# Attention row maxima folded on GpSimd and turned by a DMA through DRAM instead of by TensorE, score stream four units further ahead

## The chip, the core and the metric

One core of a Trainium2 chip runs the whole kernel. The metric is the device time of one execution in microseconds. The kernel before took 1684.84 us, the median of three runs (1678.03 to 1687.31).

## What is computed

One attention layer with a learned scale and offset, a residual layer norm, a linear layer whose input and weight are rounded blockwise to four-bit floats, and another residual layer norm. Batch 2, length 2048, width 256, 16 heads of 16 columns. The part that matters here:

```python
scores = jnp.einsum('bhqd,bhkd->bhqk', Q, K) / sqrt(DK)
scores = scores * tau[..., None] + delta[:, :, None, :]
attn = jax.nn.softmax(scores, axis=-1)
out = jnp.einsum('bhqk,bhkd->bhqd', attn, V)
```

tau and delta are folded into Q and into an extra pair of rows of K, so that one matmul gives the scores.

## The kernel before

The kernel has three stages. The first (0 to about 256 us) makes Q, K and V from x and stores Q and K in DRAM as high and low parts. The second is the attention. The third is the projection, the norms and the four-bit linear layer; a part of it already runs beside the last attention iterations, and the rest is the tail.

The attention runs NIT = 32 iterations. An iteration is one group of four heads (HG) with one chunk of 512 queries; four iterations (NQ) make a group, and at each group's start `group_load` fetches the next group's K and Q into the other half of `k_set` and `q_set`. The softmax needs each row's maximum before the exponent is taken, so the scores are made twice:

- The score stream (`s_unit`, L227) puts 128 queries by 512 keys for two heads into two PSUM banks, and `max_unit` (L237, VectorE) takes the row maxima. There are 32 such units in an iteration's work (UNITS), numbered (j, u) for iteration j. They are the list `items`, in which a few other things are mixed: the item "rows", the item "ft", and twelve output projections O (`block_of`, L867 to L870).
- The transposed scores (`st`, L924) have keys on the partitions. The negated maxima stand as two rows (high and low part) in `q_set`, so that the matmul subtracts them. ScalarE takes the exponent (L1069), and `pv_half` (L937) multiplies it by V.

The order on TensorE is written out by hand. An iteration has 32 slots (SLOTS). In each slot stand one `pv_half`, then one `st` pair for the tile two further on (AHEAD), then the score items that are due. The loop reads:

```python
goal = items.index((i + 2, LEAD)) if i + 2 < NIT else len(items) - 1
due = goal - issued
...
while issued < first + min(due, due * (2 * k + jh + 1) // slots):
    s_item(issued)
```

With LEAD = 12, iteration i ends when 12 units of iteration i + 2 have been issued. An ordinary iteration has 33 items (32 units and one "rows") for its 32 slots, so its last slot has two of them.

The maxima of iteration j go this way: after the last unit VectorE folds the four key chunks (`row_maxima`, L260), GpSimd splits them into high and low parts (`split_max`, L85 and L89), and three units later the item "rows" lets TensorE transpose the 128x128 pad (`rows_turn`, L244) and VectorE copy 32 rows out of PSUM (`rows_copy`, L252). Then SyncE issues four DMAs of 4 KB into `q_set` (`rows_store`, L278). The first `st` of iteration i + 1 is in slot 28 of iteration i and waits for these (`rows_set`).

On ScalarE, `evacuate` (L1058) copies the finished output of an iteration out of PSUM bank 0; the first `pv_half` of the next iteration waits for it (`att_evac`). GpSimd also copies V for the next group (`refill`, L1326) at the quarters of each fourth iteration, and `split_max` stands behind the second of these. It multiplies the output chunks in the end (`normalise`, L1350). SyncE's program in iteration i is: `group_load` (each fourth iteration), `att_store(i - 1)`, loads of output chunks in a few iterations, `rows_store(i + 1)`, and in iteration 30 `z_store(1)` and `next_load(4)` behind it.

In iteration 30 the last 20 units are spread over 24 slots, and slot 24 holds four pairs of unread matmuls (`unread`, L883) and the last "rows".

Of the kernel before, what the change touches and what calls it, by code (L numbers as in the profile page):

```python
# [66 lines left out]
GROUP_DMAS = 2 * (2 * TERMS + 1)  # L67
# [54 lines left out]
def layer_kernel(nc, t, out):  # L122
# [6 lines left out]
    att = dram("att", [NIT, P, CH], F32)  # L129
    z_rows = dram("z_rows", [NCHUNK, HG, HG, CH], F32)  # L130
    rz_rows = dram("rz_rows", [NCHUNK, HG, HG, CH], F32)

    with ExitStack() as top:
# [10 lines left out]
        q_set = sb(top, "q_set", [P, 2, HH, L], F32R)  # L144
# [10 lines left out]
        def group_load(eng, g, done, cols=slice(0, L)):  # L155

            b, h0 = g // (H // HG), g % (H // HG) * HG
            for n in range(GROUP_DMAS):
                half, r = n // (GROUP_DMAS // 2), n % (GROUP_DMAS // 2)
                heads = slice(h0 + HH * half, h0 + HH * (half + 1))  # L160
                base = HALF * half
                if r < 2 * TERMS:
                    dst, src, parts = (k_set, k_parts, K_PARTS) if r < TERMS else (q_set, q_parts, Q_PARTS)
                    r %= TERMS
                    eng.dma_start(dst[base + DK * r:base + DK * (r + 1), g % 2, :, cols].bitcast(F32),
                                  src[parts[r], b, heads, :, cols].rearrange("h d l -> d h l")).then_inc(done, 16)
                else:
                    eng.dma_start(k_set[base + ROW_AUG:base + ROW_AUG + 2, g % 2, :, cols].bitcast(F32),
                                  delta_parts[:, b, heads, cols]).then_inc(done, 16)
# [5 lines left out]
        LEAD = 12  # L175
        DEFER = 3
# [12 lines left out]
        items.append((NIT - 1, "rows"))  # L189
        rows_at = {j: s for s, (j, u) in enumerate(items) if u == "rows"}  # L190
        o_at = {u[1:]: s for s, (j, u) in enumerate(items) if (j, u) in [(k[0], v) for k, v in O_AT.items()]}
        PER = UNITS + 1
        SLOTS = 2 * KT
        s_bank = lambda s: 4 + 2 * (s % 2)
        warm_exp = sb(top, "warm_exp", [P, 1])
        nm = sb(top, "nm", [P, HG * TT])
        nm_pad = sb(top, "nm_pad", [P, P], F32R)
        nm_parts = nm_pad[:, 0:2 * HG * TT].rearrange("p (h t q) -> p h t q", h=HG, t=2)
        nm_rows = sb(top, "nm_rows", [2 * HG * TT, P], F32R)
        nm_max, nm_high, pad_zero, rows_set = sem("nm_max"), sem("nm_high"), sem("pad_zero"), sem("rows_set")  # L200
        ROWS_INC = 16 * HG
# [12 lines left out]
        def s_unit(pe, s):  # L214
# [4 lines left out]
            g, lo = j // NQ, j % NQ * CH  # L219
# [5 lines left out]
            for half in range(2):  # L225
                r = rows_of(half, K_S)
                last = nc.tensor.matmul(ps[:, s_bank(s) + half, :], q_set[r, g % 2, jh, lo + qt * P:lo + (qt + 1) * P],  # L227
# [11 lines left out]
        def rows_turn(pe, s):  # L239

            j, u = items[s]
            pe.wait_ge(s_free, s - 1)
            pe.wait_ge(nm_ready, j + 1)
            nc.tensor.transpose(ps[:, s_bank(s), 0:P], nm_pad[:].bitcast(F32), ident_f[:]).then_inc(s_full, 1)  # L244

        def rows_copy(dve, s):

            j, u = items[s]
            dve.wait_ge(s_full, s + 1)
# [4 lines left out]
        def row_maxima(dve, s):  # L254

            j, u = items[s]
            dve.wait_ge(s_free, s + 1)
            if j > 0:
                dve.wait_ge(nm_ready, j)
            nc.vector.tensor_reduce(nm[:], mx[:, j % 2].rearrange("p a j q c -> p (a j q) c"), AX.X, ALU.max, negate=True).then_inc(nm_max, 1)  # L260
# [1215 lines left out]
```

## Time and profile before

The profiled execution had a span of 1668.4 us from its first to its last instruction. Its whole time was not recorded beside it; the median of the three runs is 1684.84 us.

| | before |
|---|---|
| median of three runs | 1684.84 us |
| span of the profiled execution | 1668.4 us |
| TensorE matmuls busy | 1626.3 us (97%) |
| VectorE busy | 1522.9 us (91%) |
| ScalarE busy | 1311.3 us (79%) |
| GpSimd busy | 128.4 us (8%) |
| mean granted TensorE clock | 0.993 of full speed |
| chain that ended last | PE 59%, VectorE 24% |

L12 means line 12 of the kernel. In a row of the timeline the first number is the start in us from the span's first instruction, the second is how long the group lasted, and `x2` says that two instructions were put together. The square bracket at the end is idle time of the engine before it and what ended it. PE is TensorE, DVE VectorE, ACT ScalarE, POOL GpSimd, SPq SyncE's queue. Matmuls are pipelined and their ends are modelled, so for TensorE the starts are read and not the ends.

### The profile page before, as it was taken

Reading aid. Unit: us, or ns where it says so; the run is one execution under the profiler, and the core shown is the slowest. Engines: PE = TensorE matmul, PEld = TensorE weight load, DVE = VectorE, ACT = ScalarE, POOL = GpSimd, SP = SyncE. Lnnn points to the kernel's source line nnn. Section 1 sums busy time; section 2 is a strip of 40 time slices with the busy share of each in tenths; the row PEclk is TensorE's granted clock in tenths of the full one; section 3 lists DMA queues with packets and bytes.
Section 4 is the critical chain, followed back from the end, with each engine's and each line's share of the span. In section 5 each row is a group of like instructions: output and inputs, shape, how many; then the busy total and the mean of one; then the engine's idle time right before and its main releaser. Section 6 shows DMA issues by size and latency. Waiting matters only on the chain.

```text
span 1668.4 us, 33561 instructions
## 1 busy us (share of the span) xinstructions
PE 1626.3 (97%) x13884; PEld 727.6 (44%) x13884; DVE 1522.9 (91%) x1648; ACT 1311.3 (79%) x2375; POOL 128.4 (8%) x166
## 2 busy tenths in 40 slices
PE   8999998999999999999999999999999999999987
PEld 7766663333333333333333333333333343333466
DVE  5789877999999999999999999999999989898887
ACT  2876737888888888888888888888888876778645
POOL 4222223000000000000000000000010000000100
PEclk9999998999999999999999999999999999999999
DMA  3465426000600060015003300422151001010312
GB/s 113 110 177 157 124 86 122 8 8 9 86 8 8 17 76 8 12 26 70 9 8 41 56 8 8 52 45 53 39 63 30 8 8 40 12 41 10 124 59 89
DMA packets 46960, 84.72 MB, mean 51 GB/s; under 512 B 9116, under 2 KB 21020, under 8 KB 44092
## 3 DMA queue, kind: packets, MB, share of 16 engines
q1 hardware_dynamic: 44952, 82.49, 22.8%
q8 instruction: 109, 1.79, 0.5%
q14 instruction: 43, 0.35, 0.1%
q10 hardware_dynamic: 1856, 0.09, 0.1%
HBM read 51.36 MB, written 30.67 MB: 49 GB/s over the span
## 4 chain that ended last, share of the span: by engine, by line
PE 59%; DVE 24%; issue 1%; ACT 0%; ACTq 0%; POOL 0%; DVEq 0%
PE ps L937 25%; DVE mx L237 20%; PE ps L924 20%; PE ps L227 11%; PE ps L870 1%; DVE stats L1173 1%; PE ps L868 1%; PE ps L244 0%; DVE work L1221 0%; DVE work L1232 0%; PE ps L867 0%; DVE small L1216 0%; DVE mv L1179 0%; DVE scr L1225 0%; DVE work L1229 0%
## 5 line engine op out<-in xcount | busy, mean ns | idle before, releaser
L237 DVE TENSOR_REDUCE mx<-ps 128x2 f32<-128x1024 f32 x1024 | 1228.0, 1222 | 67.9 <-PE ps L227 59.6
L1069 ACT ACTIVATE e<-ps 128x512 f32<-128x512 f32 x2048 | 1109.6, 596 | 220.8 <-PE ps L924 182.7
L937 PE MATMUL ps<-e,v_grp 128*32 128x256 f32 x8192 | 656.1, 392 | 0.3 <-issue 0.3
L924 PE MATMUL ps<-q,k 52*128 52x512 f32 x2048 | 524.7, 499 | 4.1 <-PEq L355 3.8
L227 PE MATMUL ps<-k,q 50*128 50x512 f32 x2048 | 423.6, 405 | 9.5 <-DVE mx L237 6.6
L924 PEld LDWEIGHTS ps<-q,k 52*128 52x128 f32 x2048 | 199.6, 183 | 429.4 <-ACT e L1069 385.9
L937 PEld LDWEIGHTS ps<-e,v_grp 128*32 128x32 f32 x8192 | 161.9, 108 | 354.4 <-issue 204.4
L227 PEld LDWEIGHTS ps<-k,q 50*128 50x128 f32 x2048 | 197.7, 187 | 48.1 <-DVE mx L237 34.3
L684 PE MATMUL ps<-x_p,m_p 128*128 128x512 f32 x576 | 144.2, 404 | 0.0
L525 DVE SCALAR_TENSOR_TENSOR hid<-x_c,dw_w,hid 128x512 f32<-128x512 f32 x128 | 103.7, 860 | 19.0 <-ACT hid L466 19.0
L684 PEld LDWEIGHTS ps<-x_p,m_p 128*128 128x128 f32 x576 | 107.0, 190 | 31.8 <-issue 7.3
L472 ACT ACTIVATE hid<-hid 128x512 f32<-128x512 f32 x64 | 40.5, 632 | 52.3 <-DVE hid L525 51.0
L85 POOL CAST nm_pad<-nm 128x16 fp32r<-128x16 f32 x32 | 6.7, 210 | 871.7 <-DVE nm L260 871.7
L466 ACT ACTIVATE hid<-x_c,dw_b,dw_w 128x512 f32<-128x512 f32 x64 | 46.6, 804 | 0.2
L1326 POOL COPY v_grp<-v_all 128x272 f32<-128x272 f32 x32 | 13.7, 433 | 316.8 <-PE ps L937 316.8
L870 PE MATMUL ps<-wo_t,v_all 128*128 128x256 f32 x128 | 32.8, 379 | 0.0
L707 PE MATMUL ps<-hid,pw_w 128*16 128x512 f32 x128 | 30.2, 594 | 0.1
L1350 POOL TENSOR_TENSOR v_all<-v_all 128x1024 f32<-128x1024 f32 x8 | 20.3, 2540 | 117.5 <-DMA v_all<-rz_rows 117.5
L515 ACT ACTIVATE q_sp<-qx 128x512 fp32r<-128x512 f32 x16 | 10.1, 630 | 21.3 <-DVE qx L549 21.1
L698 PE MATMUL ps<-wv_p,x_p 128*128 128x256 f32 x192 | 26.8, 289 | 0.0
L990 PE MATMUL ps<-fw_p,xq_t 128*128 128x256 f32 x128 | 19.6, 310 | 7.0 <-ACT xq_t L1051 7.0
L89 POOL TENSOR_TENSOR q_sp<-qx,q_sp 128x512 fp32r<-128x512 f32 x16 | 20.5, 1282 | 73.6 <-ACT q_sp L515 73.5
(142 smaller groups left out, 623.5 us busy)
## 6 DMA issues: line engine op xcount, KB each, us to landing
k<-k_parts SPq DMA_DIRECT2D x42, 256.0 KB
q<-q_parts SPq DMA_DIRECT2D x42, 256.0 KB
k_parts<-k_sp SPq DMA_DIRECT2D x16, 512.0 KB, 4.9
q_parts<-q_sp SPq DMA_DIRECT2D x16, 512.0 KB, 3.8
att<-ev SPq DMA_DIRECT2D x32, 256.0 KB
x_c<-in_x_t SPq DMA_DIRECT2D x8, 514.0 KB, 5.3
tau_r<-tau_rows SPq DMA_DIRECT2D x16, 256.0 KB
x_in<-in_x SPq DMA_DIRECT2D x8, 512.0 KB, 3.9
```

What stands on the lines that cost most here:

```text
L227: last = nc.tensor.matmul(ps[:, s_bank(s) + half, :], q_set[r, g % 2, jh, lo + qt * P:lo + (qt + 1) * P], k_set[r, g % 2, jh, kc * CH:(kc ...
L237: nc.vector.tensor_reduce(mx[:, j % 2, :, jh, qt, kc], ps[:, b0:b0 + 2, :], AX.X, ALU.max).then_inc(s_free, 1)
L466: nc.scalar.activation(hid[:, k, c, r], x_c[:, n % 2, c, 1:1 + CH], ACT.Identity, bias=dw_b[:, k, c, r:r + 1], scale=dw_w[:, k, c, r, 1:2] ...
L472: nc.scalar.activation(hid[:, k, c, r], hid[:, k, c, r], ACT.Gelu).then_inc(gelu_done, 1)
L525: nc.vector.scalar_tensor_tensor(y_, x_c[:, n % 2, c, which:which + CH], dw_w[:, k, c, r, which:which + 1], y_, ALU.mult, ALU.add).then_in ...
L684: mm = nc.tensor.matmul(ps[:, o, :], m_p[:, kw, side, c, tap, P * o:P * (o + 1)], x_p[:, n % 2, kx_, c, tap:tap + CH], start=(m == 0), sto ...
L698: last = nc.tensor.matmul(ps[:, v_bank(n, v), D * a:D * (a + 1)], x_p[:, n % 2, kx_, c, lo:lo + P], wv_p[:, kw, c, :], start=(m == 0), sto ...
L707: last = nc.tensor.matmul(ps[32 * k:32 * k + H, TD_BANK, :], pw_w[:, k, 2 * c + r, :], hid[:, k, c, r, :], start=(j < 2), stop=(j >= 6))
L870: last = nc.tensor.matmul(dst, a_t[p][:, c, P * a:P * (a + 1)], wo_t[:, c, :], start=False, stop=(c == CT - 1))
L924: nc.tensor.matmul(ps[:, st_bank(n), :], k_set[r, g % 2, jh, kt * P:(kt + 1) * P], q_set[r, g % 2, jh, lo:lo + CH], start=True, stop=True) ...
L937: last = nc.tensor.matmul(ps[32 * h:32 * (h + 1), 0, PVW * part:PVW * (part + 1)], v_grp[:, kt, h, :], e[:, x % E_BUFS, h * CH + PVW * par ...
L1069: nc.scalar.activation(e[:, x % E_BUFS, h * CH:(h + 1) * CH], ps[:, st_bank(n), :], ACT.Exp).then_inc(e_ready, 1)
```

## The change

The item "rows" goes away, with its transpose on TensorE, its copy on VectorE and the fold on VectorE. GpSimd folds the four maxima of each row with small `tensor_scalar` instructions on 128x1 columns (`FOLD_ORDER`: eight places, four instructions each, and a wait in each place), then splits high and low as before into a pad of 128x32. One DMA writes the pad to DRAM turned, that is in 4096 runs of four bytes, and after waiting for it SyncE issues two DMAs that read 8 KB each back into `q_set`, whose layout becomes [rows, group, chunk, head, 512] so that these two rows are contiguous. `group_load` now has one DMA for each head of Q, in all 20 DMAs instead of 14 for a group. LEAD goes from 12 to 16. Iteration 30 spreads its units over 20 slots, without the unread matmuls. `z_reciprocal(1)` moves behind two small aggregations.

```diff
-        LEAD = 12
-        DEFER = 3
+        LEAD = 16
...
-                if u == DEFER - 1 and j > 0:
-                    items.append((j - 1, "rows"))
...
+        def split_max(pool, j):
+
+            folds = 2 * HH * TT * j
+            for qt, jh in FOLD_ORDER:
+                pool.wait_ge(s_free, unit_at[j, qt, jh, NQ - 1] + 1)
+                for half in range(2):
+                    r, parts = (half * HH + jh) * TT + qt, mx[:, j % 2, half, jh, qt]
+                    nc.gpsimd.tensor_scalar(mn[:, r:r + 1], parts[:, 0:1], parts[:, 1:2], parts[:, 2:3], ALU.max, ALU.max).then_inc(mx_folded, 1)
+                folds += 2
+                pool.wait_ge(mx_folded, folds)
+                for half in range(2):
+                    r, parts = (half * HH + jh) * TT + qt, mx[:, j % 2, half, jh, qt]
+                    nc.gpsimd.tensor_scalar(nm[:, r:r + 1], mn[:, r:r + 1], parts[:, 3:4], -1.0, ALU.max, ALU.mult).then_inc(nm_max, 1)
+            pool.wait_ge(nm_max, folds)
             if j > 0:
-                dve.wait_ge(rows_set, j * ROWS_INC)
-            nc.vector.tensor_copy(nm_rows[:], ps[0:2 * HG * TT, s_bank(s), 0:P]).then_inc(s_free, 1)
...
+                pool.wait_ge(rows_out, 16 * j)
+            cols = nm[:].rearrange("p (a r) -> p a r", a=2)
             high(nc.gpsimd, nm_parts[:, :, 0], cols).then_inc(nm_high, 1)
             pool.wait_ge(nm_high, j + 1)
             low(nc.gpsimd, nm_parts[:, :, 1], cols, nm_parts[:, :, 0]).then_inc(nm_ready, 1)
 
         def rows_store(sp, j):
 
-            sp.wait_ge(s_free, rows_at[j] + 1)
-            g, lo = j // NQ, j % NQ * CH
-            for h in range(HG):
-                row = HALF * (h // HH) + ROW_MAX
-                sp.dma_start(q_set[row:row + 2, g % 2, h % HH, lo:lo + CH].bitcast(F32).rearrange("t (a l) -> t a l", a=TT),
-                             nm_rows[h * 2 * TT:(h + 1) * 2 * TT, :].bitcast(F32)).then_inc(rows_set, 16)
+            sp.wait_ge(nm_ready, j + 1)
+            g = j // NQ
+            sp.dma_start(max_rows[j].rearrange("r p -> p r"), nm_pad[:].bitcast(F32), allow_slow_non_contiguous=True).then_inc(rows_out, 16)
+            sp.wait_ge(rows_out, 16 * (j + 1))
+            for half in range(2):
+                row = HALF * half + ROW_MAX
+                sp.dma_start(q_set[row:row + 2, g % 2, j % NQ].bitcast(F32),
+                             max_rows[j, BLOCK // 2 * half:BLOCK // 2 * (half + 1)].rearrange("(t j q) p -> t j (q p)", t=2, j=HH)).then_inc(rows_set, 16)
...
-                        if s == len(items) - 1:
-                            pe.wait_ge(s_free, s - 1)
-                            unread(s_bank(s), 4)
-                        if u == "rows":
-                            rows_turn(pe, s)
-                        else:
-                            s_unit(pe, s)
+                        s_unit(pe, s)
...
-                        goal = items.index((i + 2, LEAD)) if i + 2 < NIT else len(items) - 1
+                        goal = items.index((i + 2, LEAD)) if i + 2 < NIT else len(items)
                         due = goal - issued
-                        slots = SLOTS * 3 // 4 if i == NIT - 2 else SLOTS
+                        slots = SLOTS * 5 // 8 if i == NIT - 2 else SLOTS
```

## Rows read from the trace of the kernel before

**Rows 1.** The page: the chain that ended last, shares of the span by engine.
```profile
PE 59%; DVE 24%; issue 1%; ACT 0%; ACTq 0%; POOL 0%; DVEq 0%
```

**Rows 2.** Instructions of line L1058 up to 1200 us: count, ns min/median/max, first and last start.
```profile
L1058 ACT ACTIVATE ev<-ps x23: 602/603/604, 303.8 to 1194.0; 128x512 f32<-128x512 f32 x23
```

**Rows 3.** Timeline of TensorE, iteration from 627.6 to 667.85: start us, us, what.
```profile
656.09 0.64 PE L937 MATMUL ps<-e,v_grp 128*32 128x256 f32 x8
...
657.35 0.64 PE L937 MATMUL ps<-e,v_grp 128*32 128x256 f32 x8
...
658.59 0.64 PE L937 MATMUL ps<-e,v_grp 128*32 128x256 f32 x8
659.16 0.51 PE L924 MATMUL ps<-q,k 52*128 52x512 f32 x2
659.50 0.41 PE L227 MATMUL ps<-k,q 50*128 50x512 f32 x2
...
666.03 0.64 PE L937 MATMUL ps<-e,v_grp 128*32 128x256 f32 x8
...
666.93 0.98 PE L227 MATMUL ps<-k,q 50*128 50x512 f32 x4
667.85 0.64 PE L937 MATMUL ps<-e,v_grp 128*32 128x256 f32 x8
```

**Rows 4.** Timeline of VectorE, an ordinary iteration and a stretch with a backlog.
```profile
658.70 35.28 DVE L237 TENSOR_REDUCE mx<-ps 128x2 f32<-128x1024 f32 x29 [0.96 <-PE ps L227]
...
1377.87 9.24 DVE L237 TENSOR_REDUCE mx<-ps 128x2 f32<-128x1024 f32 x8 [0.43 <-PE ps L227]
```

**Rows 5.** Timeline of ScalarE where two iterations meet.
```profile
666.92 0.60 ACT L1058 ACTIVATE ev<-ps 128x512 f32<-128x512 f32 x1
```

**Rows 6.** Timeline of TensorE, iteration 30: two slots that hold one score unit.
```profile
1514.38 0.64 PE L937 MATMUL ps<-e,v_grp 128*32 128x256 f32 x8
...
1516.85 0.64 PE L937 MATMUL ps<-e,v_grp 128*32 128x256 f32 x8
```

**Rows 7.** Timeline of TensorE, iteration 31: two slots without any score item.
```profile
1573.55 0.64 PE L937 MATMUL ps<-e,v_grp 128*32 128x256 f32 x8
...
1575.80 0.64 PE L937 MATMUL ps<-e,v_grp 128*32 128x256 f32 x8
```

**Rows 8.** Timeline of TensorE, iteration 30: the last "rows" slot, then an output projection.
```profile
1536.68 0.64 PE L937 MATMUL ps<-e,v_grp 128*32 128x256 f32 x8
...
1539.21 0.64 PE L937 MATMUL ps<-e,v_grp 128*32 128x256 f32 x8
...
1542.43 0.28 PE L867 MATMUL ps<-bias,ones 128*128 128x256 bf16 x1
...
1543.94 0.64 PE L937 MATMUL ps<-e,v_grp 128*32 128x256 f32 x8
```

**Rows 9.** The page: DMA queues, with packets, MB and share of 16 engines' span.
```profile
q1 hardware_dynamic: 44952, 82.49, 22.8%
q10 hardware_dynamic: 1856, 0.09, 0.1%
```

**Rows 10.** Instructions of tile z (loads of 32 KB from DRAM): issue to landing.
```profile
DMA to landing us min/median/max: 1.7/1.8/2.9
```

**Rows 11.** Timeline of GpSimd, iteration 3, which began at 385.25.
```profile
404.57 0.43 POOL L1326 COPY v_grp<-v_all 128x272 f32<-128x272 f32 x1 [9.49 <-PE ps L937]
411.70 0.20 POOL L85 CAST nm_pad<-nm 128x16 fp32r<-128x16 f32 x1 [6.69 <-DVE nm L260]
411.98 0.23 POOL L89 TENSOR_TENSOR nm_pad<-nm,nm_pad 128x16 fp32r<-128x16 f32 x1
```

**Rows 12.** Busy us of each engine at a group load's end; clock, DMA share, GB/s last.
```profile
445.00:450.00 5.00, 5.00 (x50) 1.82 (x48) 4.74 (x5) 4.17 (x9) 0.00 (x0) 1.00 0.54 98
```

**Rows 13.** Timeline of TensorE, iteration 31: the first block of projection 4.
```profile
1558.56 0.27 PE L867 MATMUL ps<-bias,ones 128*128 128x256 bf16 x1 [1.04 <-issue]
```

**Rows 14.** Timeline of VectorE, the start of the tail.
```profile
1597.62 0.76 DVE L1173 BATCH_NORM_STATS2 stats<-ps 128x6 f32<-128x256 f32 x2 [5.28 <-PE ps L870]
```

More of the change, by code:

```diff
@@ L66 @@
 THREE = ((0, 0), (0, 1), (1, 0))
-GROUP_DMAS = 2 * (2 * TERMS + 1)
+GROUP_DMAS = 2 * (TERMS + HH * TERMS + 1)
 def chain(eng, sem, base=0):
@@ L188, in layer_kernel @@
                     items.append((j, O_AT[j, u]))
-        items.append((NIT - 1, "rows"))
-        rows_at = {j: s for s, (j, u) in enumerate(items) if u == "rows"}
+        FOLD_ORDER = [(qt, jh) for qt in range(TT) for jh in range(HH)]
         o_at = {u[1:]: s for s, (j, u) in enumerate(items) if (j, u) in [(k[0], v) for k, v in O_AT.items()]}
-        PER = UNITS + 1
         SLOTS = 2 * KT
@@ L195, in layer_kernel @@
         warm_exp = sb(top, "warm_exp", [P, 1])
+        mn = sb(top, "mn", [P, HG * TT])
         nm = sb(top, "nm", [P, HG * TT])
[L197 to L201, printed above, removed]
+        nm_pad = sb(top, "nm_pad", [P, BLOCK], F32R)
+        nm_parts = nm_pad[:].rearrange("p (a t r) -> p a t r", a=2, t=2)
+        mx_folded, nm_max, nm_high, rows_out, rows_set = sem("mx_folded"), sem("nm_max"), sem("nm_high"), sem("rows_out"), sem("rows_set")
+        ROWS_INC = 16 * 2
         mx = sb(top, "mx", [P, 2, 2, HH, TT, NQ])
@@ L226, in s_unit @@
                 r = rows_of(half, K_S)
-                last = nc.tensor.matmul(ps[:, s_bank(s) + half, :], q_set[r, g % 2, jh, lo + qt * P:lo + (qt + 1) * P],
+                last = nc.tensor.matmul(ps[:, s_bank(s) + half, :], q_set[r, g % 2, j % NQ, jh, qt * P:(qt + 1) * P],
                                         k_set[r, g % 2, jh, kc * CH:(kc + 1) * CH], start=True, stop=True)
@@ L712, in pre_scores @@
                     for s in pre_at.get((n, place), ()):
-                        if items[s][1] == "rows":
-                            rows_turn(pe, s)
-                        else:
-                            s_unit(pe, s)
+                        s_unit(pe, s)
                 beta(1, 0)
@@ L876, in loaded @@
                         pe.wait_ge(a_norm, n + 1)
-                    def unread(bank, pairs):
-                        for m in range(pairs):
-                            for half in range(2):
-                                r = rows_of(half, K_S)
-                                nc.tensor.matmul(ps[:, bank + half, :], q_set[r, (NG - 1) % 2, 0, 0:P], k_set[r, (NG - 1) % 2, 0, 0:CH], start=True, stop=True)
                     def s_item(s):
@@ L1012, in _ @@
                                     issued += 1
-                                if i == NIT - 2 and 2 * k + jh == slots:
-                                    s_item(len(items) - 1)
                             if x in PROJECT_AT:
```

72 lines of the change are left out of this document (22 added, 50 removed).

## The prediction, made before the changed kernel was run

> **What bounds the kernel now.** I read the page first. Its busy shares, 97% for TensorE and 91% for VectorE, are too near each other to decide anything; the chain that ended last gives 59% to the one and 24% to the other [rows 1]. The copies of the finished output mark the iterations: 23 of them from 303.8 to 1194.0 us, so 890.2 / 22 = 40.46 us for an iteration [rows 2]. The timeline of TensorE says what one is made of. A slot with one score unit lasts 658.59 - 657.35 = 1.24 us, the slot with the transpose 657.35 - 656.09 = 1.26, and the last slot, which has two units, 667.85 - 666.03 = 1.82 [rows 3]. The sum 30 x 1.24 + 1.26 + 1.82 = 40.28 is the iteration.
>
> Is VectorE the pace of the 1.24? Its 29 reduces in 35.28 us are 1.217 each, nearly without idle time, and look like a bound. But where it has a backlog, eight take 9.24 us, 1.155 each [rows 4]. It could do 32 reduces in 37.0 us. So VectorE follows TensorE, except in the two-unit slot, where the second pair stands 0.5 us behind the first (four matmuls last 0.98 us where a pair lasts 0.41 [rows 3]), since a PSUM pair comes free only after a reduce. What the change takes from VectorE (a fold and a copy for each iteration) is therefore worth nothing by itself in the ordinary iterations. What counts is TensorE's list of slots.
>
> **The edge between iterations.** One item fewer makes 32 items for 32 slots, and no slot has two. I don't take that as 1.82 down to 1.24, for the next `pv_half` also waits for the output copy: it starts at 666.92 and takes 0.60, to 667.52 [rows 5]. With 0.05 for the handover (an assumption, no row gives it) TensorE could go on at 667.57 and not at 667.85. So the edge slot becomes 667.57 - 666.03 = 1.54, a gain of 0.28. Its bounds are 0, should something else hold it, and 0.58. The transpose slot becomes a plain one and gives 0.02. That is 0.30 an iteration, at most 0.6, at least 0.02.
>
> **The sum over iterations.** I worked out from the two lists how many items fall in each iteration.
> - Iterations 1 to 23: 33 items become 32. 23 x 0.30 = 6.9 us gained.
> - Iteration 0: 36 items become 38 because of LEAD, four two-unit slots become six. An extra one costs 1.82 - 1.24 = 0.58. Lost: 1.2.
> - Iteration 24 loses one two-unit slot (34 to 33, 0.6) and iteration 25 is ordinary (0.3). Gained: 0.9.
> - Iteration 26 gets a second output projection and loses "rows". A projection takes 1543.94 - 1542.43 = 1.51 in its slot [rows 8], where a score pair takes 1.24 - 0.91 = 0.33 [rows 3]. Lost: 1.2.
> - Iterations 27 and 28: 37 become 36, one two-unit slot fewer each, with VectorE near its limit. Gained: 0.9 each (0.6 from TensorE's side, 1.2 if a reduce's whole time counts), 1.8.
> - Iteration 29: 36 become 34 with one projection fewer. Two two-unit slots (1.2) and a projection (1.2). Gained: 2.4.
> - Iteration 30: the slot with the unread matmuls and the last transpose took 1539.21 - 1536.68 = 2.53 [rows 8] and becomes one without a score item. Leaving a unit out of a slot gives nothing while every second slot has one: 1516.85 - 1514.38 = 2.47 for two slots with one unit [rows 6], the same as 2 x 1.24, since ScalarE then catches up. Only where no units are left is a slot shorter, 2.25 / 2 = 1.12 [rows 7]. The last units end in slot 19, not 23, so four slots at 0.12 and one at 1.4. Gained: 1.9.
> - The tail gives nothing. It begins where VectorE had been idle 5.28 us for the last projection but two [rows 14], so it moves with TensorE.
> - The first stage has 42 units in place of 41 and a transpose ahead of the attention, 0.1 us. The new `rows_store(0)` there blocks SyncE for some 5 us ahead of two stores, whose data GpSimd and ScalarE give later anyway. Nothing.
>
> Together 6.9 - 1.2 + 0.9 - 1.2 + 1.8 + 2.4 + 1.9 = 11.5 us gained, if nothing comes late.
>
> **Does the new path come in time?** The slots are counted from an iteration's start. The first `st` of the next iteration stands in slot 28, 28 x 1.24 = 34.7 us in, and 659.16 - 658.59 = 0.57 behind the slot's start (the score pair is 0.91 behind it) [rows 3]. So the rows are due at 35.3 us.
>
> *The last unit.* With LEAD = 16 it is in slot 15: 15 x 1.24 + 0.91 = 19.5, matmul 0.4 [rows 3], reduce 1.2 [rows 4], so its maxima stand at 21.2.
>
> *GpSimd.* The trace shows no fold of 128x1 there. The nearest rows are a cast of 128x16 at 0.20 and the instruction that waits for it, 0.28 behind [rows 11]. Two folds, a wait and two folds I put at 0.75; it may be 0.45 or, if reading two scalars from SBUF is slow, 1.3. The last place then ends at 21.9, and high and low add 0.6: 22.6. The other seven places are done by then. What is queued behind the waits on GpSimd is the refill for the next group, and there the order matters: in iterations 3, 7, ... 27 `split_max` stands behind the second refill, which began 404.57 - 385.25 = 19.3 in and took 0.43 [rows 11]. All eight places come after 19.8, so 19.8 + 8 x 0.75 + 0.6 = 26.5 (24.0 to 30.8).
>
> *The DMA out.* 4096 runs over 16 engines are 256 for each. No row shows it. The nearest is queue 10, which moved small pieces: 0.1% of 16 engines' span is 26.7 us for 1856 packets, 14 ns each, and by the rounding 7 to 22 [rows 9]. The far end is queue 1, 22.8% for 44952 packets of 1.8 KB, 135 ns each. With 1.7 us for what any small DMA takes [rows 10] the DMA is 5.4 us, between 3.5 and 36. I take 5.4, since queue 10's packets are the nearest in size, and see its own spread of 3.5 to 7.4 as likely.
>
> The Trainium skill, "DMA: Bandwidth & Descriptors", gives about 10.5 ns for a packet (Measured) and about 2 us fixed (Anatomy of one DMA), so an estimate of 2.0 + 256 x 10.5 ns = 4.7 us; the sum would be the same by it.
>
> *The two DMAs in.* An issue of 0.6 each and a landing of 1.8 behind the second's start [rows 10]: 2.4.
>
> So an ordinary iteration has its rows at 22.6 + 5.4 + 2.4 = 30.4, due 35.3; the DMA out may take up to 10.3. A group's last iteration has them at 34.3, and the DMA out may take up to 6.4. In iteration 30 the last unit is in slot 19, four slots later, 5.0 us: rows at 35.4 against 20 x 1.24 + 8 x 1.12 + 0.57 = 34.3. That one is late by 1.1 us. SyncE, blocked meanwhile, has behind it `z_store(1)` and `next_load(4)`, for whose outcome TensorE waited 1.04 us already [rows 13]; but by this reckoning it comes free at 34.2, about a microsecond sooner than now. I charge 1.0 for iteration 30.
>
> *Queues.* The load of group 2 kept the DMA engines busy for 0.54 of the stretch from 445 to 450 [rows 12], so it ended about 447.7. The iteration began at 385.25 + 40.3 = 425.5, so that is 22.2 us in; its bytes stay, its Q pieces shrink from 8 to 2 KB. The DMA out would be issued at 22.7, right behind. Should the load grow by two or three of the 4.9 us to spare there, nothing is late. The 20 issues for 14 are 3 us more of SyncE, beside the transfers.
>
> Total: 11.5 - 1.0 = 10.5 us gained. The span of 1668.4 becomes 1657.9. The change touches nothing outside the span, so I take the same off the median: 1684.8 - 10.5 = 1674.3 us.
>
> **Rivals.**
> - *Late at the groups' ends only.* The DMA out takes about 8.5 us, or the folds 1.1 a place. Then 8.5 - 6.4 = 2.1 us in seven iterations is 14.7, and iteration 30 loses 4.2 and not 1.0. In all 11.5 - 18.9 = 7.4 lost: 1692. With 7.5 us it is 11.5 - 7.7 - 3.2 = 0.6 gained: 1684. For it: 256 little writes to DRAM for each engine are seen nowhere in the trace. Against it: queue 10.
> - *The DMA out is slow everywhere, and the kernel slower.* The place is `rows_out` on SyncE, the point from which it decides is 10.3 us (34 ns a piece). At 13 us it costs 2.7 x 23 = 62 in ordinary iterations, 6.6 x 7 = 46 at the groups' ends and 8.7 in iteration 30, so 105 lost and 1790. Beyond it every microsecond costs 31. The row for it is queue 1 with 135 ns a packet, against it that those are big packets. The skill's page "DMA: Bandwidth & Descriptors" speaks against the change here: a strided last dimension becomes one descriptor for each element, and its rules for kernel authors call a plain DMA with a rearranged pattern, as a transpose, 19 times slower than the hardware's. No run here shows that ratio.
> - *The edge gives nothing.* Something else keeps the edge at 1.82, or the chain through ScalarE's copy shifts. Then 0.28 x 25 = 7.0 fall away: 3.5 gained, 1681.
>
> **How the numbers follow.** Forecast, in time nearly everywhere: 0.57, with 1668 to 1679 for its own range (edge gain 0.58 at one end, iteration 0 and the projections worse at the other, and the spread of the runs). Late at the groups' ends: 0.16. Slow everywhere: 0.14. Edge gives nothing: 0.13. The range must leave out the slow case and little more: 1667 to 1693. About 0.5%, 8.4 us, is what a measurement of this kernel can tell from no change. Below 1676.4 lies some three quarters of the forecast's case: 0.44. Above 1693.3 lie the slow case and a part of the late one: 0.18. Between them 0.38.
>
> **What would show each step.** In the profile after: two starts of L937 across an edge 1.54 us apart, ordinary iterations of 40.0 us, no pair of units in a slot. VectorE with idle time in each slot's end, which costs nothing. GpSimd with 32 small instructions an iteration, 0.75 us a place. The DMA out at 5.4 us between its issue and the issues of the two DMAs in. The wait of the first `st` in slot 28 absent, but for iteration 30. I am wrong if that wait shows in iterations 3, 7, ... 27 (late folds or DMA), or in all, or if slots without two units last longer than 1.24.

## The result: 2067 us, a fifth slower

The changed kernel takes 2067.40 us, the median of four runs (2059.09 to 2095.76), beside 1685.64 us (1678.03 to 1687.31), the median of four for the kernel before. The ratio is 1.228, with a 95% interval of 1.2237 to 1.2326; the slow one of the four, 2095.76 us at a lower granted clock, is left out of it. The forecast was 1674.3 us with a range of 1667 to 1693, so both were wrong. The case that happened is the rival "the DMA out is slow everywhere", to which I had given 0.14 and a price of 1790 us.

| | before | after |
|---|---|---|
| median of four runs | 1685.64 us | 2067.40 us |
| span of the profiled execution | 1668.4 us | 2057.2 us |
| TensorE matmuls busy | 1626.3 us (97%) | 1767.3 us (86%) |
| VectorE busy | 1522.9 us (91%) | 1525.1 us (74%) |
| GpSimd busy | 128.4 us (8%) | 450.6 us (22%) |
| mean granted TensorE clock | 0.993 | 0.871 |

The page of the changed kernel: number of packets, then the chain that ended last by engine and by line. Line numbers are those of the changed kernel: L264 is the DMA out, L268 the two in, L891 `st`, L904 `pv_half`, L225 the score units.
```profile
DMA packets 182614, 85.29 MB, mean 41 GB/s; under 512 B 141628, under 2 KB 152508, under 8 KB 181084
...
PE 32%; DMA 27%; DVE 19%; POOL 6%; issue 1%; ACT 1%; SPq 0%; POOLq 0%; ACTq 0%; DVEq 0%
DMA max_rows<-nm_pad 24%; DVE mx L235 16%; PE ps L904 14%; PE ps L891 11%; PE ps L225 6%; DMA q<-max_rows 4%; POOL mn L246 3%; POOL nm L251 2%; PE ps L850 1%; DVE stats L1133 1%; PE ps L848 1%; SPq L268 0%; POOL nm_pad L89 0%; POOL nm_pad L85 0%; DVE work L1192 0%
```
In [rows 1] no DMA stood in the chain. Now the DMA out alone has 24% of it. The group of `st` on the page shows the wait (busy us, mean ns, then idle time before it and what ended it):
```profile
L891 PE MATMUL ps<-q,k 52*128 52x512 f32 x2048 | 577.0, 545 | 255.1 <-DMA q<-max_rows 243.5
L904 PE MATMUL ps<-e,v_grp 128*32 128x256 f32 x8192 | 723.2, 428 | 1.1 <-ACT ev L1023 0.8
```
One ordinary iteration, 592.20 to 641.16 us, shows how it goes. SyncE's queue:
```profile
615.80 0.38 SPq L264 DMA_DIRECT2D max_rows<-nm_pad  x1
630.96 0.53 SPq L268 DMA_DIRECT2D q<-max_rows  x2
```
The DMA out is issued 23.6 us into the iteration, and the two DMAs in follow 15.16 us later. Over the 32 iterations this distance is 14.65 to 17.2 us, median 15.75. TensorE, where the iteration's first `st` for the next iteration stands:
```profile
626.04 0.64 PE L904 MATMUL ps<-e,v_grp 128*32 128x256 f32 x8
...
627.51 0.64 PE L904 MATMUL ps<-e,v_grp 128*32 128x256 f32 x8
633.53 0.79 PE L891 MATMUL ps<-q,k 52*128 52x512 f32 x2 [5.38 <-DMA q<-max_rows]
634.68 1.08 PE L904 MATMUL ps<-e,v_grp 128*32 128x256 f32 x8
...
636.85 1.08 PE L904 MATMUL ps<-e,v_grp 128*32 128x256 f32 x8
...
639.00 1.08 PE L904 MATMUL ps<-e,v_grp 128*32 128x256 f32 x8
```
The wait is 5.38 us, and the slots behind it last 636.85 - 634.68 = 2.17 us and not 1.24. The same stretch by engine busy time; the last three columns are granted clock, DMA share and GB/s:
```profile
616.00:618.00 2.00, 2.00 (x24) 0.68 (x22) 1.97 (x3) 1.86 (x4) 0.00 (x0) 1.00 0.48 8
...
622.00:624.00 2.00, 2.00 (x24) 0.61 (x20) 1.97 (x3) 1.69 (x5) 0.00 (x0) 1.00 0.22 0
...
626.00:628.00 2.00, 2.00 (x22) 0.79 (x20) 1.75 (x3) 1.80 (x4) 0.00 (x0) 1.00 0.00 0
...
633.00:638.00 5.00, 4.47 (x26) 1.55 (x26) 2.27 (x2) 2.17 (x4) 0.00 (x0) 0.50 0.00 1
638.00:643.00 5.00, 5.00 (x28) 1.75 (x28) 2.63 (x3) 2.77 (x5) 0.00 (x0) 0.50 0.14 54
643.00:648.00 5.00, 5.00 (x46) 1.58 (x44) 4.11 (x4) 3.95 (x8) 0.00 (x0) 0.88 0.00 0
```
Three things are to be seen. The packets of the DMA out are over by 626, yet SyncE is released only at 631: the records of its packets end long before the DMA counts as done. Nor are these records long. From 614 to 634 us the queue that carries it shows (packets, MB, share of 16 engines' time):
```profile
q1 hardware_dynamic: 4120, 0.03, 17.3%
```
That is 0.173 x 16 x 20 us / 4120 = 13.4 ns a packet, next to the 14 ns that the prediction took from queue 10. By its packet records the DMA out is as cheap as forecast; what takes the time is not in them. And behind the wait TensorE has a granted clock of 0.50, 1.2 GHz in place of 2.4, up to about 644 (0.88 is the mean of a stretch that begins at 0.50).

### The profile page after: what moved, and what is told of

Its sections match the earlier page's. It is cut to its first block, busy times and chain, and to the rows that moved or that the text cites. A ratio compares the mean times of both kernels' runs of the same rounds, so it can differ in the third digit from the quotient of the medians.

```text
span 2057.2 us, 34377 instructions
## 1 busy us (share of the span) xinstructions
PE 1767.3 (86%) x13839; PEld 763.4 (37%) x13844; DVE 1525.1 (74%) x1584; ACT 1315.1 (64%) x2375; POOL 450.6 (22%) x1189
## 4 chain that ended last, share of the span: by engine, by line
PE 32%; DMA 27%; DVE 19%; POOL 6%; issue 1%; ACT 1%; SPq 0%; POOLq 0%; ACTq 0%; DVEq 0%
DMA max_rows<-nm_pad 24%; DVE mx L235 16%; PE ps L904 14%; PE ps L891 11%; PE ps L225 6%; DMA q<-max_rows 4%; POOL mn L246 3%; POOL nm L251 2%; PE ps L850 1%; DVE stats L1133 1%; PE ps L848 1%; SPq L268 0%; POOL nm_pad L89 0%; POOL nm_pad L85 0%; DVE work L1192 0%
## 5 line engine op out<-in xcount | busy, mean ns | idle before, releaser
L235 DVE TENSOR_REDUCE mx<-ps 128x2 f32<-128x1024 f32 x1024 | 1241.7, 1224 | 429.3 <-PE ps L225 417.4
L891 PE MATMUL ps<-q,k 52*128 52x512 f32 x2048 | 577.0, 545 | 255.1 <-DMA q<-max_rows 243.5
L904 PE MATMUL ps<-e,v_grp 128*32 128x256 f32 x8192 | 723.2, 428 | 1.1 <-ACT ev L1023 0.8
L891 PEld LDWEIGHTS ps<-q,k 52*128 52x128 f32 x2048 | 218.1, 199 | 747.0 <-ACT e L1034 446.3
L225 PE MATMUL ps<-k,q 50*128 50x512 f32 x2048 | 458.1, 438 | 6.5 <-DVE mx L235 6.2
L246 POOL TENSOR_SCALAR mn<-mx 128x1 f32<-128x1 f32 x512 | 182.4, 365 | 698.8 <-DVE mx L235 676.1
L904 PEld LDWEIGHTS ps<-e,v_grp 128*32 128x32 f32 x8192 | 168.4, 112 | 413.2 <-issue 269.9
L225 PEld LDWEIGHTS ps<-k,q 50*128 50x128 f32 x2048 | 221.4, 209 | 32.4 <-DVE mx L235 18.8
L251 POOL TENSOR_SCALAR nm<-mn,mx 128x1 f32<-128x1 f32 x512 | 141.5, 290 | 25.2
L1286 POOL COPY v_grp<-v_all 128x272 f32<-128x272 f32 x32 | 13.5, 428 | 502.1 <-PE ps L904 502.1
L89 POOL TENSOR_TENSOR q_sp<-qx,q_sp 128x512 fp32r<-128x512 f32 x16 | 20.5, 1280 | 73.9 <-ACT q_sp L503 73.7
L89 POOL TENSOR_TENSOR x_p<-x_c,x_p 128x1028 fp32r<-128x1028 f32 x8 | 19.3, 2415 | 63.2 <-ACT x_p L448 63.1
L1023 ACT ACTIVATE ev<-ps 128x512 f32<-128x512 f32 x32 | 19.1, 598 | 15.6 <-PE ps L904 15.6
```

What stands on the lines that cost most here:

```text
L235: nc.vector.tensor_reduce(mx[:, j % 2, :, jh, qt, kc], ps[:, b0:b0 + 2, :], AX.X, ALU.max).then_inc(s_free, 1)
L246: nc.gpsimd.tensor_scalar(mn[:, r:r + 1], parts[:, 0:1], parts[:, 1:2], parts[:, 2:3], ALU.max, ALU.max).then_inc(mx_folded, 1)
L251: nc.gpsimd.tensor_scalar(nm[:, r:r + 1], mn[:, r:r + 1], parts[:, 3:4], -1.0, ALU.max, ALU.mult).then_inc(nm_max, 1)
L891: nc.tensor.matmul(ps[:, st_bank(n), :], k_set[r, g % 2, jh, kt * P:(kt + 1) * P], q_set[r, g % 2, i % NQ, jh, :], start=True, stop=True). ...
L904: last = nc.tensor.matmul(ps[32 * h:32 * (h + 1), 0, PVW * part:PVW * (part + 1)], v_grp[:, kt, h, :], e[:, x % E_BUFS, h * CH + PVW * par ...
```

## The experiments

All are edits of the changed kernel but for three, where that is said. "DMA out" is the distance from its issue to the issue of the first DMA in behind it, median of the 32; a slot is the distance between two successive groups of eight `pv_half` matmuls. A slot is called long when it is 0.8 to 1.1 us over 1.24 after all waits of its `st` are taken off. Where no range stands, the time is that of one run.

### 1. The same bytes in runs of 128

```diff
-            sp.dma_start(max_rows[j].rearrange("r p -> p r"), nm_pad[:].bitcast(F32), allow_slow_non_contiguous=True).then_inc(rows_out, 16)
+            sp.dma_start(max_rows[j].rearrange("r p -> (r p)").rearrange("(p r) -> p r", p=P), nm_pad[:].bitcast(F32)).then_inc(rows_out, 16)
...
-                                nc.scalar.activation(e[:, x % E_BUFS, h * CH:(h + 1) * CH], ps[:, st_bank(n), :], ACT.Exp).then_inc(e_ready, 1)
+                                nc.scalar.activation(e[:, x % E_BUFS, h * CH:(h + 1) * CH], ps[:, st_bank(n), :], ACT.Exp, scale=2.0**-10).then_inc(e_ready, 1)
```

> The changed kernel with one thing other: the DMA out writes each partition's 32 maxima as one run of 128 bytes (128 runs), not turned, so that the two DMAs in fetch misplaced maxima; the exponent's scale is lowered so that it stays finite. All counts of instructions and bytes stay. Theory: the four-byte writes are the whole loss. Then DMA out to the next issue falls from 15.2 us to 1.7 to 2.5, ordinary iterations come to 40.0 us with an edge of 1.54, and the groups' last iterations are about 1 us late, since eight places of 1.43 us on GpSimd end at 31.9 us. Time 1674 plus 7 x 1 us, and up to 7 x 5 more if the TensorE clock falls after such a wait: 1675 to 1715. Rival: a part of the loss is in the rest of the change (more DMAs for the group load, folds on GpSimd, 16 units ahead): then well above 1715.

Measured: 1664.41 us (1662.9 to 1670.38) beside 1677.37, ratio 0.9915 (0.9886 to 0.9944). SyncE's queue in one iteration, then the copies of the finished output up to 1200 us:
```profile
651.84 0.35 SPq L264 DMA_DIRECT2D max_rows<-nm_pad  x1
653.28 0.54 SPq L268 DMA_DIRECT2D q<-max_rows  x2
```
```profile
L1023 ACT ACTIVATE ev<-ps x23: 603/603/603, 306.8 to 1190.0; 128x512 f32<-128x512 f32 x23
```
The DMA out takes 653.28 - 651.84 = 1.44 us, no `st` waits for rows, and an iteration lasts (1190.0 - 306.8) / 22 = 40.15 us in the mean, against 40.46 in [rows 2]. So the whole loss, 2057.2 - 1662.5 = 394.7 us of span, comes from the shape of one DMA of 16 KB. GpSimd's folds, the blocked SyncE, the finer loads of Q and the longer lead together cost nothing that shows here. That wrong maxima pass through this kernel does not explain it: experiment 7, whose result is right, has the same iterations.

The 394.7 us can be taken apart by slots. From the first to the last slot the changed kernel takes 1724.6 us and this one 1330.8, 393.8 more. Of these, 248.5 are waits of `st`: 243.5 for rows, the others for ScalarE. 115.1 - 4.7 = 110.4 are long slots (125 of them against 5), the 2.17 us slots above. The rest, 35, are smaller and larger lengthenings.

### 2. The size of the runs

The same 16 KB in 2048 runs of 8 bytes, again not turned. In this, in 3 and in 5 the exponent has the scale of experiment 1.

```diff
+            sp.dma_start(max_rows[j].rearrange("r p -> (r p)").rearrange("(r p w) -> p r w", p=P, w=2), nm_pad[:].bitcast(F32).rearrange("p (r w) -> p r w", w=2)).then_inc(rows_out, 16)
```

> The changed kernel with 2048 runs of eight bytes in place of 4096 of four (misplaced maxima, lowered exponent scale). If each little write has its price, about 57 ns on its engine, the DMA out falls from 15.2 us to about 8.5 and the ordinary iterations meet their due time or miss it by little: 1690 to 1760. If the price is by bytes or is fixed for a turned pattern, it stays at 15 us and the time above 2000.

Measured: 1726.14 us, DMA out 7.28. The first `st` waits only where a group of heads ends, 4.5 to 5.0 us in six of them and 2.2 in iteration 27, and 1.7 us in iteration 30 (the waits of TensorE: us in total, times, longest):
```profile
PE ps L891 <- DMA q<-max_rows: 32.5, 8, 5.0
```
This puts a point between the two thresholds of the prediction, 6.4 and 10.3 us: 7.28 us is in time in ordinary iterations and late at the groups' ends.

### 3. Four bytes, 64 bytes apart

The contiguous DMA of experiment 1 feeds the kernel, and beside it the pad goes out turned as in the change, but each run to a 64-byte piece of its own.

```diff
+            sp.dma_start(max_far[j, :, :, 0].rearrange("r p -> p r"), nm_pad[:].bitcast(F32), allow_slow_non_contiguous=True).then_inc(rows_out, 16)
```

> The changed kernel, but the 4096 runs of four bytes go to places 64 bytes apart in another DRAM tensor, and a contiguous copy beside it feeds the DMAs in (misplaced maxima, lowered exponent scale). Rival theory: the writes are slow since sixteen of them, from different engines, hit the same 64-byte piece of DRAM. By it the DMA out falls from 15 us to below 8. By the theory of a price for each write it stays at 15 to 16 us, time 2040 to 2100.

Measured: 1741.14 us, 8.22 us for both DMAs (6.3 to 10.4), waits of 5.5 to 7.5 us at the groups' ends (2.4 at the last). As many runs as in the changed kernel, of the same size, take half the time once no two share 64 bytes. No other spacing was run, and the runs are also spread over sixteen times as much memory, so that 64 bytes is the size that counts is not shown.

### 4. The turn on the way in

The pad goes out contiguous, and four DMAs of 1024 four-byte pieces each read it turned. Nothing is left out.

```diff
-                sp.dma_start(q_set[row:row + 2, g % 2, j % NQ].bitcast(F32),
...
+                for part in range(2):
+                    c0 = BLOCK // 2 * half + BLOCK // 4 * part
+                    sp.dma_start(q_set[row + part:row + part + 1, g % 2, j % NQ].bitcast(F32).rearrange("t j (q p) -> t (j q) p", p=P),
+                                 max_rows[j, :, c0:c0 + BLOCK // 4].rearrange("p r -> r p").unsqueeze(0), allow_slow_non_contiguous=True).then_inc(rows_set, 16)
```

> The changed kernel with the turn on the other side: out as 128 runs of 128 bytes, and in by four DMAs whose 1024 pieces of four bytes each are read from DRAM with a stride and written to SBUF in order, on eight engines, so 512 for an engine. The result is the full one. If a four-byte write to DRAM is the dear thing and a four-byte read and a write into SBUF are cheap (7 to 14 ns), out takes 2 us and in 6 to 10 us, and the time is 1675 to 1720. If any four-byte piece costs 57 ns, in takes 29 us and the time goes beyond 2200.

Measured: 2260.57 us. `st` waits 450.2 us in all, and the issues alone hold SyncE for 10 us:
```profile
PE ps L893 <- DMA q<-max_rows: 450.2, 32, 22.6
```
```profile
654.37 0.32 SPq L264 DMA_DIRECT2D max_rows<-nm_pad  x1
655.78 10.27 SPq L270 DMA_DIRECT2D q<-max_rows  x4
```
The first `st` behind these came at 676.29, 20.5 us behind the first issue. Reading in four-byte pieces is no way out.

### 5. Neighbours written one behind the other

After experiment 3 my theory was that several DMA engines meet in one 64-byte piece of DRAM. Here each partition's 128 bytes are meant to be written by one engine, in order, still as 4-byte runs. For this the pad in SBUF holds its values 8 bytes apart, so the reading side changes too.

```diff
-        nm_pad = sb(top, "nm_pad", [P, BLOCK], F32R)
-        nm_parts = nm_pad[:].rearrange("p (a t r) -> p a t r", a=2, t=2)
+        nm_pad = sb(top, "nm_pad", [P, BLOCK, 2], F32R)
+        nm_parts = nm_pad[:, :, 0].rearrange("p (a t r) -> p a t r", a=2, t=2)
...
-            sp.dma_start(max_rows[j].rearrange("r p -> p r"), nm_pad[:].bitcast(F32), allow_slow_non_contiguous=True).then_inc(rows_out, 16)
+            sp.dma_start(max_rows[j].rearrange("r p -> (r p)").rearrange("(p r) -> p r", p=P), nm_pad[:, :, 0].bitcast(F32), allow_slow_non_contiguous=True).then_inc(rows_out, 16)
```

> The changed kernel with 4096 runs of four bytes, read with a stride of eight from the pad and written in order, so that each partition's 128 bytes of DRAM are written by one engine (misplaced maxima, lowered exponent scale). Runs to places 64 bytes apart took 8.2 us with the copy beside them, runs next to each other from several engines 15.8. If the second half of the price comes from several engines writing one 64-byte piece, this one takes 6 to 8.5 us and the time is 1710 to 1760. If it comes from writing the same piece sixteen times by whatever engine, it stays at 14 to 16 and the time above 2000.

Measured: 2516.8 us, the slowest of all. SyncE's queue, and three of the stretches behind the issue (last columns: clock, DMA share, GB/s; a share can pass 1, since the records of packets overlap):
```profile
658.07 0.56 SPq L264 DMA_DIRECT2D max_rows<-nm_pad  x1
687.55 0.53 SPq L268 DMA_DIRECT2D q<-max_rows  x2
```
```profile
663.00:668.00 5.00, 5.00 (x52) 1.83 (x48) 4.94 (x5) 4.38 (x9) 1.25 (x4) 1.00 1.58 1
...
673.00:678.00 5.00, 0.00 (x0) 0.00 (x0) 0.00 (x0) 0.00 (x0) 0.00 (x0) 0.66 0.05 0
678.00:683.00 5.00, 0.00 (x0) 0.00 (x0) 0.00 (x0) 0.00 (x0) 0.00 (x0) 0.50 0.00 0
```
The theory fell. As the DMA is written, no 64-byte piece is shared between engines (the trace does not name the engine of a packet), and it takes 28.75 us, not less. From 678 us on no packet is in the records, nearly ten of the 29.5 us of this one. With the contiguous 1.44 us taken off, and the runs taken as spread evenly over 16 engines, the price of one run on its engine is:

| what is written | runs per engine | DMA out | ns a run |
|---|---|---|---|
| 4 B, next run in the same 64 B (this one) | 256 | 28.75 us | 107 |
| 4 B turned (the change) | 256 | 15.75 us | 56 |
| 8 B (experiment 2) | 128 | 7.28 us | 46 |
| 16 B (experiment 7) | 64 | 3.15 us | 27 |
| 4 B, 64 B apart (experiment 3; 0.38 us for the second issue taken off too) | 256 | 8.22 us | 25 |

So the price is not one of a packet's passage. Among the four-byte runs it is lowest where no two share 64 bytes and highest where they follow each other into the same 64. What in the memory path does it stays open, and for the 107 ns so does the part of the spaced reading from SBUF, which was not tried alone. The Trainium skill, "DMA: Bandwidth & Descriptors" (Specifications), says that below 512 bytes the DMA reads, modifies and writes. That would fit a run that has to wait for its neighbour, but it doesn't by itself tell 25 ns from 107, and no run here shows the reading.

### 6. The late start on GpSimd

In the iterations that end a group, the eight folds stand behind the second refill. This takes that away, with all work kept.

```diff
-                            if c == 2 and i + 1 < NIT:
+                            if c == 0 and i + 1 < NIT:
```

> The changed kernel with GpSimd's fold and split put ahead of the refills for the next group instead of behind the second one. Theory: in iterations 3, 7, ... 27 the eight places, 1.43 us each, stand behind a refill that begins at 19.3 us, which makes the stall 15 us there instead of 5.5. Then those seven stalls fall to 5 to 6 us and the time by 7 x 9.5 = 66 us, to 1985 to 2015. Rival: the DMA out is later there for another cause, and the time stays above 2050.

Measured: 2033.48 us. The waits at the groups' ends fall to about 6 us, as long as those of ordinary iterations:
```profile
PE ps L891 <- DMA q<-max_rows: 187.7, 32, 10.2
```
That is 243.5 - 187.7 = 55.8 us less waiting, near the 66 expected, but only 25.6 us less span, so the time missed its range. The long slots rose from 115.1 to 147.3 us; two traces of the changed kernel itself differ by 21 (136.2 in experiment 9). So the mechanism of the wait is right, and shorter waits did not bring fewer slots at the lower clock.

### 7. Sixteen bytes, the turn half done by the matmul

From the kernel before. A unit takes the queries 4p + qt and not qt * 128 + p, by a strided read of its weights, so four maxima of a partition lie together in a row and the DMA out has 1024 runs of 16 bytes. The fold stays on VectorE, LEAD is 14, nothing is left out.

```diff
-                last = nc.tensor.matmul(ps[:, s_bank(s) + half, :], q_set[r, g % 2, jh, lo + qt * P:lo + (qt + 1) * P],
+                last = nc.tensor.matmul(ps[:, s_bank(s) + half, :], q_set[r, g % 2, jh, lo:lo + CH].rearrange("r (p q) -> r p q", q=TT)[:, :, qt],
...
+            sp.dma_start(max_rows[j].rearrange("r p q -> p r q"), nm_pad[:].bitcast(F32).rearrange("p (r q) -> p r q", q=TT)).then_inc(rows_out, 16)
```

> A kernel of its own, full result: the kernel before without the item rows; VectorE folds as before; unit qt takes the queries 4p + qt (weights read with a stride of 16 bytes), so that a partition's four maxima are neighbours in the row and the turn through DRAM needs 1024 runs of 16 bytes; LEAD = 14, last units over 20 slots. If a little write costs 46 to 57 ns, 64 for each engine are 3 to 3.7 us and the DMA out is 4.4 to 5.1, in time everywhere. The slots are those of the contiguous run, less one two-unit slot in iteration 0: 1660 to 1668, 0.85% to 1% below the kernel before. Against it: if the strided weights load slower than the matmul before hides, each slot grows from 1.24 and the time is above 1690.

Measured: 1668.01 us (1666.4 to 1672.04) beside 1679.17, ratio 0.9935 (0.9914 to 0.9956).
```profile
658.16 0.37 SPq L255 DMA_DIRECT2D max_rows<-nm_pad  x1
661.36 1.25 SPq L259 DMA_DIRECT2D q<-max_rows  x2
```
The DMA out takes 3.15 us in the median, no `st` waits for rows, ordinary iterations last 40.0 us, and a slot is 1.24 with the strided weights as without. This kernel is 0.65% below the kernel before, a small gain but clear of the noise, and far below the changed one.

### 8. Its lead, and the lead alone

The same with LEAD = 12:

> The variant with runs of 16 bytes, with the score stream at the changed kernel's least lead that still covers the rows: 12 units in place of 14. Its two DMAs take 3.15 us out and about 2 in where the rows would then land some 32.6 us into an iteration and are wanted at 35.3. Theory: nothing waits in ordinary iterations, the first iteration saves two slots (1.2 us), and the time is 1664 to 1670 us, as with 14. Rival: at the ends of the groups of heads the rows come 4 us later and now too late; then a wait of about 1.3 us and the clock behind it, in 7 iterations, 1678 to 1690 us.

Measured: 1673.12 us (1668.64 to 1676.31) beside 1676.78, ratio 0.9968 (0.9948 to 0.9987). No wait for rows in ordinary iterations or at groups' ends, as the theory had it, but no gain either; against 0.9935 the intervals overlap.

And the kernel before with its lead changed and nothing else:

```diff
-        LEAD = 12
+        LEAD = 16
```

> The kernel before with LEAD = 16 and nothing else: the score stream four units ahead, the turn still on TensorE. Iteration 0 has 40 items for 36 and pays 4 x 0.58 = 2.3 us; the last iterations get back as much; the edge keeps its two units. Expected the same within 0.3% of the kernel before. If the stream's lead were the gain seen with the contiguous DMA (14 us), it would show here.

Measured: 1675.48 us beside 1679.17, ratio 0.9977 (0.995 to 1.0004): no difference that can be told.

### 9. Is the rest the clock?

The changed kernel with matmuls that nobody reads ahead of the wait for the rows, in two sizes, and once as it is.

```diff
+                            if i > 0:
+                                n_next = filler_at[0]
+                                pe.wait_ge(s_free, min(n_next, len(items)) - 1)
+                                for m in range(62 if i % NQ == 0 else 22):
+                                    for half in range(2):
+                                        r = rows_of(half, K_S)
+                                        nc.tensor.matmul(ps[:, s_bank(n_next) + half, :], q_set[r, g % 2, 0, 0, 0:P], k_set[r, g % 2, 0, 0:CH], start=True, stop=True)
```

First with 45 and 15:

> The changed kernel, all of its work kept, with matmuls that nobody reads put in front of the wait of the first st for its rows (15 pairs in an ordinary iteration, 45 where a new group of heads begins), so that TensorE computes while the rows are on their way. In the changed kernel that wait takes 4.5 to 7.8 us in an ordinary iteration and 13.5 to 15.5 at a group's first, 244 us in all, and beside it some 150 us more are lost against the kernel with runs of 128 bytes. Theory: these 150 us are TensorE at 1.2 GHz after each idle wait (slots of 2.16 us at a granted clock of 0.50 where 1.24 is usual). Then the slots behind the wait stay at 1.24 us, the period of an ordinary iteration falls from 49 to 52 us to about 46, and the time to 1920 to 1950 us. Rival: the slots are long for another reason, the rows' packets in the DMA engines or a backlog of VectorE; then the filled wait changes nothing and the time stays at 2040 or above.

Measured: 2076.59 us, so by the letter the rival's number. But the trace says something else than the rival: the mean clock rose to 0.916, the long slots fell from 115.1 to 79.5 us, and the DMA out took 17.62 us and not 15.75, which is 1.9 x 31 = 59 us by itself. The fill was too short as well. This was inconclusive, hence two more (the 77 us of the second text are these 79.5, counted with only the wait for the rows taken off):

> The changed kernel as it is, on the same chip as the run with the longer filled wait beside it. With 15 and 45 pairs of unread matmuls ahead of the wait, the DMA out took 17.6 us in place of 15.75 and the time did not fall. If that is the chip it ran on, the DMA out of the changed kernel is about 17 us here and its time 2100 us or more. If the unread matmuls lengthen it, it is 15 to 16.5 us here and the time 2060 to 2075 us.

> The changed kernel with 22 pairs of unread matmuls ahead of the wait in an ordinary iteration and 62 at a group's first (15 and 45 before), enough to cover nearly the whole wait. At 0.43 us a pair they take 9.5 and 26.7 us, more than the waits of the changed kernel, so the time is no lower: 2030 to 2110 us. What is asked is the clock. Theory (the slots of 2.16 us follow from the idle wait): with 15 and 45 pairs 77 us were left in slots 0.8 to 1.1 us too long, after 115 in the changed kernel and 5 in the kernel with runs of 128 bytes; now under 20 us are left, and the mean granted clock is 0.97 or more. Rival: such slots come with the scattered DMA whether TensorE waits or not; then 60 us or more of them stay.

Measured on one chip: the changed kernel 2072.98 us with a DMA out of 15.56, the one with the filled wait 1971.73 us with 15.70. TensorE of the latter in an ordinary iteration, and its clock there:
```profile
610.20 0.64 PE L911 MATMUL ps<-e,v_grp 128*32 128x256 f32 x8
610.90 5.30 PE L891 MATMUL ps<-k,q 50*128 50x512 f32 x44
616.01 0.42 PE L898 MATMUL ps<-q,k 52*128 52x512 f32 x2
616.60 0.64 PE L911 MATMUL ps<-e,v_grp 128*32 128x256 f32 x8
...
617.83 0.64 PE L911 MATMUL ps<-e,v_grp 128*32 128x256 f32 x8
```
```profile
610.00:615.00 5.00, 4.94 (x46) 3.74 (x46) 1.97 (x2) 0.71 (x2) 0.00 (x0) 1.00 0.04 7
615.00:620.00 5.00, 5.00 (x52) 2.51 (x48) 3.27 (x3) 3.17 (x7) 0.00 (x0) 1.00 0.00 0
```
Here L891 is the unread matmuls, L898 `st` and L911 `pv_half`. The rows come as late as before. But TensorE's clock stays at 1.00 and the next slot is 617.83 - 616.60 = 1.23 us. What is left of idle waiting for the rows in the whole kernel (us in total, times, longest):
```profile
PE ps L898 <- DMA q<-max_rows: 20.1, 11, 4.7
```
The long slots fall from 136.2 us (the changed kernel on this chip) to 31.5, and the time falls by 2072.98 - 1971.73 = 101 us by work that nobody needs, one run beside one run. The rival, 60 us or more, is out; the theory's own marks, under 20 us and a mean clock of 0.97, were not quite reached (31.5 and 0.966), and some waits were left unfilled. The theory of the clock stands. My price of the fill was wrong: 22 pairs took 5.3 us, 0.24 a pair and not 0.43, so it did not overrun the wait and the time fell, where I had expected it to stay.

The unread matmuls don't lengthen the DMA out, since 15.70 stands beside 15.56. What did so in the first try is likely its chip: the 16-byte DMA of experiment 8, which ran beside it, took 3.37 us against 3.15 on another chip. With 1.44 taken off both are 13% longer. That was not tested further.

## Why the prediction was wrong, step by step

- *TensorE is the pace, VectorE follows.* Right. With the DMA mended (experiment 1), slots are 1.24 us and VectorE's fold and copy are gone without a gain of their own: experiment 7 keeps the fold on VectorE and has iterations of 40.0 us too.
- *The edge becomes 1.54.* Right. In experiment 1 two `pv_half` groups across an edge start at 627.04 and 628.60, 1.56 us apart, the second with 0.24 us of waiting for ScalarE's copy, as reckoned from [rows 5]. Ordinary iterations came to 40.0 us.
- *The sum.* Its parts 1 to 25 held: 22 iterations gained 890.2 - 883.2 = 7.0 us, reckoned 22 x 0.30 = 6.6. The first copy came 3.0 us later (306.8 for 303.8), of which I had charged 1.2 for iteration 0. Iterations 29 and 30 gained 2.4 and 1.9 as reckoned. Iterations 27 and 28 lost 0.6 and 3.2 where I had a gain of 1.8 in all; in 28 a slot of 3.8 us is followed by slots of 2.16, the clock again. Between the first copy and the last the gain is 1295.7 - 1286.8 = 8.9 us. In the whole span of the two traces it is 5.9 us, and by the ratio of 0.9915 it is 14 us on 1684.8 (9 to 19); my 11.5 lies in the latter.
- *GpSimd's place of 0.75 us.* Mis-sized, beyond even the 1.3 that I had as its upper end. One place, then eight behind one another, of which the first and the last stand here:
```profile
613.85 0.70 POOL L246 TENSOR_SCALAR mn<-mx 128x1 f32<-128x1 f32 x2 [3.60 <-DVE mx L235]
614.65 0.55 POOL L251 TENSOR_SCALAR nm<-mn,mx 128x1 f32<-128x1 f32 x2
615.27 0.20 POOL L85 CAST nm_pad<-nm 128x16 fp32r<-128x16 f32 x1
...
662.25 0.71 POOL L246 TENSOR_SCALAR mn<-mx 128x1 f32<-128x1 f32 x2
663.05 0.55 POOL L251 TENSOR_SCALAR nm<-mn,mx 128x1 f32<-128x1 f32 x2
...
671.60 0.71 POOL L246 TENSOR_SCALAR mn<-mx 128x1 f32<-128x1 f32 x2
```
 A place is (671.60 - 662.25) / 7 = 1.34 us. In an ordinary iteration that is 0.6 us more, at a group's end 8 x 0.59 = 4.7. So the DMA out may take 10.3 - 0.6 = 9.7 us, and at the groups' ends 6.4 - 4.7 = 1.7.
- *The DMA out of 5.4 us.* The step that failed. It takes 15.75. I took 14 ns a run from the packet records of queue 10 [rows 9], "the nearest in size", and counted them as the whole price. The packet records of this DMA are 13.4 ns each too, but until it counts as done a run costs 56 ns on its engine; the step took the records' time for the DMA's. The far end of 36 us did hold it, but I had narrowed the own spread to 3.5 to 7.4 (its upper end is 7.3 by its own terms), which is the rounding of queue 10's share alone, without a row that excluded more.
- *The thresholds.* Right in kind, and with the place of 1.34 us right in size too. The waits should be 15.75 - 9.7 = 6.1 us in ordinary iterations and 15.75 - 1.7 = 14.1 at groups' ends; they are 4.2 to 8.1 and 13.5 to 15.5 (10.6 in iteration 27), and 10.4 in iteration 30. With 8 bytes it is 7.28 - 1.7 = 5.6 (measured 4.5 to 5.0), with pieces of their own 8.22 - 1.7 = 6.5 (5.5 to 7.5), and the contiguous one, at 1.44, is in time by 0.3.
- *What no step had: the clock.* 23 x 6.1 + 7 x 14.1 is 239 us, and `st` waited 243.5 with iteration 30. The reckoning then gives 1684.8 - 11.5 + 243.5 = 1917 us. The other 145 to 150 us are mainly TensorE at 1.2 GHz behind each wait: 110 of them stand in long slots, and experiment 9 gets 101 back. The rival "slow everywhere" had the place right, but by its own rule of 31 us for each microsecond a DMA out of 15.75 us gives only 1790 + 2.75 x 31 = 1875 us; it lacked the dearer place on GpSimd and the clock.
- *The rule that spoke against the change.* The same 16 KB took 15.75 us turned and 1.44 contiguous, 10.9 times as long. In kind this agrees with the rule of the Trainium skill that the prediction cites against the change. The 10.5 ns a packet of the Trainium skill, "DMA: Bandwidth & Descriptors" (Measured), is near the 13.4 ns of the packet records here, but it does not carry over to the time of these writes, where the runs show 25 to 107 ns a run.

## What to carry to other kernels

A DMA that turns a small tile through DRAM is priced by its writes, and a four-byte run beside others just written costs several times what its packet shows in the trace. Give the runs 16 bytes or more, for instance by choosing which rows a matmul takes, or let TensorE turn the tile. The busy share of the DMA engines does not tell how long such a DMA takes; the distance from its issue to what waits for it does. And where a wait on TensorE is reckoned, the slots behind it have to be reckoned too: here some 145 us more went with 244 us of waiting, most of it TensorE at 1.2 GHz.

## What the hardware showed that I had not expected

- The records of DMA packets end long before the writes are done: in the changed kernel by 626 where SyncE is released at 631 us, in experiment 5 over nine microseconds ahead.
- Four-byte writes that follow each other into the same 64 bytes came dearer (107 ns a run) than those scattered 64 bytes apart (25 ns), in one run each.
- Behind a wait of 5.38 us TensorE was granted 0.50 from 633 to about 644 us, while it was busy throughout; with the wait filled by unread matmuls it was granted 1.00.
- A `tensor_scalar` of 128x1 on GpSimd takes 290 to 365 ns, while a cast of 128x16 beside it takes 200 [rows 11].
- A strided read of a matmul's weights, 16 bytes apart, cost nothing in the slot.
